# A selective scan that fetches its rows of C from memory instead of spreading them with TensorE

## The chip, the cores and the metric

The kernel runs on one core of a Trainium2 chip. The metric is the device time of one execution in microseconds (us). In this text PE is TensorE, DVE is VectorE, ACT is ScalarE, POOL is GpSimd and SP is the engine that here only issues DMAs. SBUF is the on-chip memory of 128 partitions, PSUM the memory that PE writes to, in eight banks of 512 float32 numbers per partition.

## The reference

Eight layers work one after the other on an activation x, seen here as 32 tiles of 128 tokens by 128 numbers. The change is in the fifth, a state-space layer. Cut to what it touches, per token t, channel d (256 channels) and state n (16 states):

```
xdbl = xc @ W_xproj                  # gives dt_r, B (16 numbers), C (16 numbers) per token
dt = softplus(dt_r @ W_dt + b_dt)
A = -exp(A_log)
h[t] = h[t-1] * exp(dt[t] * A) + dt[t] * B[t] * u[t]      # u is xc
y[t] = sum over n of h[t, n] * C[t, n]
out = x + ((y + xc * D_param) * silu(z)) @ W_out
```

All of it is float32.

## The kernel before, in words

The scan stage is the function `selective_scan` (L2628 to L3209). Tokens lie along the free dimension, channels on the partitions: 256 channels are two halves of 128 (`CH` = 2), and the tokens are cut into B = 8 groups q of S = 512, each with two sequences of 256. One turn m = 16 q + n handles state n of group q, so there are M = 128 turns, and nearly every operation of a turn is on 128 partitions by 1024 numbers. A turn has these steps:

1. SP fetches row n of B of the group from a scratch tensor in memory (`b_rows`) into all 128 partitions (L2707), 256 KB, into a ring of NB = 4 tiles `bs`. Before turn m it waits until the product of turn m - 4 is done.
2. POOL multiplies `dBu = du * bs` (L2770), into a ring of ND = 3, so it can be three turns ahead of the recurrence.
3. ACT computes the decay `dA = exp(dt * A)` in two calls (L2914) into PSUM banks 0 to 3, two turns ahead at most.
4. DVE runs the recurrence `h = dA * h + dBu` with one scan instruction (L3015), into a ring of NH = 5. One operand is in PSUM and one in SBUF.
5. h is weighed with row n of C. PE spreads that row to all partitions: it multiplies `pick`, a selection matrix, by `bc`, which holds B and C split into three bfloat16 parts whose sum is the float32 value (`spread`, L3122). The result is in PSUM bank 4 (`c_bank`), a single buffer, so the next spread waits until the weighing before it has read the bank. In 13 turns of 16, DVE weighs (`weigh`, L3024), with h in SBUF and C in PSUM. In turns with n = 0, 3 and 6, ACT copies the bank to SBUF (`take_c`, L2820) and POOL weighs (L2717), four turns later.
6. PE adds the weighed h to two PSUM banks `y_bank` through the identity matrix (`add_up`, L3139). The weighed tiles are in rings of NC = 3 (DVE's) and 2 (POOL's).

Every engine works through a list in a fixed order, with semaphores between them. DVE's order is recurrence m + 1, then weighing m, and once in each group `finish` (L3030) and `add` (L3036). POOL's is product m, then what the group needs once, then the weighing of m - 4 if it is POOL's.

Once in each group, work for the next ones is put between the turns: convolution, projection to B, C and the step sizes, gating, output. `take_bc` (L2859) on ACT copies the 32 rows of B and C out of PSUM to `raw` and stores the 16 rows of B to memory. The split into three parts takes three steps on ACT (`split_first` L2875, `split_mid` L2879, `split_done` L2883 and L2884) and two subtractions on POOL (`split_left` L2722, `split_last` L2726). The matrix `pick` is prepared on POOL in the first layer (L2615), ahead of the layer's own work for the next groups. `keep_running` (L3152) issues matmuls that serve no result. Each layer ends with a barrier over all engines.

Of the kernel before, what the change touches and what calls it, by code (L numbers as in the profile page):

```python
# [17 lines left out]
P = 128  # L18
# [2563 lines left out]
class ScanWeights:  # L2582
# [4 lines left out]
    def __init__(self, chip, ctx):  # L2587
        sb = lambda name, shape, dt=F32: chip.sb(ctx, f"scan_{name}", shape, dt)
        self.packed, self.w_dt = sb("packed", [P, self.WIDTH]), sb("w_dt", [R, DI])
        self.w_tap, self.pick = sb("w_tap", [P, TAPS, DI]), sb("pick", [P, N, P], BF16)  # L2590
# [37 lines left out]
def selective_scan(chip, held, answers):  # L2628
# [3 lines left out]
    PART = 32  # L2632
    NA, NB, ND, NH, NC = 2, 4, 3, 5, 3
# [3 lines left out]
    with ctx:  # L2637
# [5 lines left out]
        pick, d_diag, a_neg = held.pick, held.d_diag, held.a_neg  # L2643
# [9 lines left out]
        raw, dtr, left, mid = sb("raw", [2 * N, S]), sb("dtr", [R, S]), sb("left", [2 * N, S]), sb("mid", [2 * N, S], BF16)  # L2653
        bc = two("bc", [P, S], BF16)
        bs = [sb(f"bs{k}", [P, S]) for k in range(NB)]
        dBu, h, hc = ([sb(f"{n}{k}", [P, CH, S]) for k in range(c)] for n, c in (("dBu", ND), ("h", NH), ("hc", NC)))
        hp, c_rows = two("hp", [P, CH, S]), two("c_rows", [P, S])
        hp_ready, c_copied = sem("hp_ready"), sem("c_copied")
        dA = [chip.banks[:, CH * k:CH * (k + 1), :] for k in range(NA)]
        c_bank, y_bank = chip.psum[4], chip.psum[5:7]  # L2660
        b_rows = nc.dram_tensor("l2a_b_rows", (B, N, S), F32, kind="Internal").ap()
# [11 lines left out]
        for q in range(B):  # L2673
# [11 lines left out]
        xc_ready, sz_ready, hi_ready, raw_ready, left_ready, mid_ready, left2_ready, bc_ready = (  # L2685
            sem(n) for n in ("xc_ready", "sz_ready", "hi_ready", "raw_ready", "left_ready", "mid_ready", "left2_ready", "bc_ready"))
        log_ready, dt_ready, du_ready, exp_order = sem("log_ready"), sem("dt_ready"), sem("du_ready"), sem("exp_order")
        b_stored, edges = sem("b_rows_stored"), sem("edges_zeroed")
        b_loaded = [sem(f"b_loaded{k}") for k in range(NB)]
        dA_ready, dBu_ready, h_ready, C_ready, hc_ready, hc_summed, yT_ready = (  # L2690
            sem(n) for n in ("dA_ready", "dBu_ready", "h_ready", "C_ready", "hc_ready", "hc_summed", "yT_ready"))
        dve_order, cleared = sem("dve_order"), sem("bc_cleared")
# [4 lines left out]
        with nc.Block(no_gpsimd_drain=True) as block:  # L2697
            @block.sync
            def _(sp):
                answers.load(sp, (0,))  # L2700
                for m in range(M):
                    q, n = divmod(m, N)
                    if n == 0:
                        sp.wait_ge(b_stored, 16 * (q + 1))
                    if m >= NB:
                        sp.wait_ge(dBu_ready, m - NB + 1)
                    sp.dma_start(bs[m % NB][:], b_rows[q, n, :].partition_broadcast(P)).then_inc(b_loaded[m % NB], 16)  # L2707

            @block.gpsimd
            def _(pool):  # L2710
                def weigh(m):
                    k = pool_no[m]
                    pool.wait_ge(c_copied, k + 1)
                    pool.wait_ge(h_ready, m + 1)
                    if k >= 2:
                        pool.wait_ge(hc_summed, add_no[of_pool[k - 2]])
                    pool.tensor_tensor(hp[k % 2][:], h[m % NH][:], bcast(c_rows[k % 2][:], n_before=CH), ALU.mult).then_inc(hp_ready, 1)  # L2717

                def split_left(q):
                    pool.wait_ge(hi_ready, q + 1)  # L2720
                    pool.wait_ge(raw_ready, q + 1)
                    pool.tensor_tensor(left[:], raw[:], bc[q % 2][0:2 * N, :], ALU.subtract).then_inc(left_ready, 1)  # L2722

                def split_last(q):
                    pool.wait_ge(mid_ready, q + 1)
                    pool.tensor_tensor(left[:], left[:], mid[:], ALU.subtract).then_inc(left2_ready, 1)  # L2726
# [34 lines left out]
                split_left(0)  # L2761
                split_last(0)
                for m in range(M):
# [9 lines left out]
                    if q + 1 < B:  # L2773
                        if n == (5 if q else 7):
                            split_left(q + 1)
                        if n == 10:
                            split_last(q + 1)
# [8 lines left out]
            def _(act):  # L2786
# [27 lines left out]

                def take_c(m):
                    k = pool_no[m]
                    act.wait_ge(C_ready, m + 1)
                    if k >= 2:
                        act.wait_ge(hp_ready, k - 1)
                    act.copy(c_rows[k % 2][:], c_bank[:]).then_inc(c_copied, 1)  # L2820
# [38 lines left out]
                def take_bc(q):  # L2859
                    job = ("bc", q)  # L2860
                    bk.wait_filled(act, job, 0)
                    if q:
                        act.wait_ge(left2_ready, q)
                    act.copy(dtr[:], ps(job)[2 * N:2 * N + R, :]).then_inc(dtr_ready, 1)
                    if q:
                        act.wait_ge(b_stored, 16 * q)
# [3 lines left out]
                    act.dma_start(b_rows[q], raw[0:N, :]).then_inc(b_stored, 16)  # L2870

                def split_first(q):
                    if q >= 2:
                        act.wait_ge(C_ready, (q - 1) * N)
                    act.copy(bc[q % 2][0:2 * N, :], raw[:]).then_inc(hi_ready, 1)  # L2875

                def split_mid(q):
                    act.wait_ge(left_ready, q + 1)
                    act.copy(mid[:], left[:]).then_inc(mid_ready, 1)  # L2879

                def split_done(q):
                    act.wait_ge(left2_ready, q + 1)
                    act.copy(bc[q % 2][PART:PART + 2 * N, :], mid[:])  # L2883
                    act.copy(bc[q % 2][2 * PART:2 * PART + 2 * N, :], left[:]).then_inc(bc_ready, 1)  # L2884

# [43 lines left out]
                act.wait_ge(cleared, 1)  # L2929
                split_first(0)  # L2930
# [4 lines left out]
                split_mid(0)  # L2935
# [5 lines left out]
                split_done(0)  # L2941
                for m in range(M):
# [3 lines left out]
                    if m in pool_no:  # L2946
                        take_c(m)
# [6 lines left out]
                    if q + 1 < B:  # L2954
                        if n == 0 + late:
                            take_bc(q + 1)
                        if n == 1 + late:
                            split_first(q + 1)
# [4 lines left out]
                        if n == 6 + late:  # L2963
                            split_mid(q + 1)
                        if n == 7 + late:
                            log_dt(q + 1)
                        if n == 11 + late:
                            split_done(q + 1)
# [15 lines left out]
            def _(dve):  # L2984
# [33 lines left out]
                def weigh(m):  # L3018
                    k = dve_no[m]
                    dve.wait_ge(C_ready, m + 1)  # L3020
# [3 lines left out]
                    dve.tensor_tensor(hc[k % NC][:], h[m % NH][:], bcast(c_bank[:], n_before=CH), ALU.mult).then_inc(hc_ready, 1)  # L3024
# [14 lines left out]
                for u in range(2):  # L3039
                    ins = dve.memset(bc[u][:], 0.0)  # L3040
                ins.then_inc(cleared, 1)
# [32 lines left out]
            def _(pe):  # L3074
# [37 lines left out]
                def spread(m):  # L3112
                    if m >= M:
                        return
                    q, n = divmod(m, N)
                    if n == 0:
                        pe.wait_ge(bc_ready, q + 1)
                    if m - 1 in dve_no:
                        pe.wait_ge(hc_ready, dve_no[m - 1] + 1)
                    if m - 1 in pool_no:  # L3120
                        pe.wait_ge(c_copied, pool_no[m - 1] + 1)
                    pe.matmul(c_bank[:], pick[:, n, :], bc[q % 2][:], start=True, stop=True).then_inc(C_ready, 1)  # L3122

# [33 lines left out]
                keep_running(6, c_bank)  # L3157
# [5 lines left out]
                keep_running(1, c_bank)  # L3163
# [5 lines left out]
                keep_running(5, c_bank)  # L3169
                spread(0)  # L3170
                for m in range(M):
# [5 lines left out]
                    spread(m + 1)  # L3177
# [145 lines left out]
```

## Time and profile before

| | |
|---|---|
| median of 3 runs | 2709.16 us (2704.49 to 2710.79) |
| the profiled execution's own time | 2704.73 us |
| its span | 2703.0 us |
| busy over the span: PE, DVE, POOL, ACT | 2478.8, 1738.7, 1617.9, 1451.4 us |
| mean granted clock of TensorE | 0.959 |

The span is the time from the first to the last instruction, and busy time is time in which an engine executes something. Busy times of the engines overlap. The scan stage is about a sixth of the span, from the first product on POOL (L2770) at 834.13 us to the last weighing, which ends at 1269.02 us. A line of a group shows engine, operation, output and inputs with their shapes, the number of instructions, their busy time in us, the mean duration of one in ns, and after the second bar the idle time of the engine just before them and what ended it.

### The profile page before, as it was taken

What the parts mean: (1) busy time and instruction counts of PE and PEld (TensorE: products, weight loads), DVE (VectorE), ACT (ScalarE), POOL (GpSimd) and SP (SyncE); (2) the same over time, 40 slices, a digit from 0 to 9 for tenths busy, and PEclk for the clock granted to TensorE, in tenths of its full rate; (3) what the DMA queues carried; (4) which work ended last, traced back from release to release, by engine and by line L of the source; (5) the groups of instructions that cost most, each with busy time, mean ns of one, the idle gap of its engine ahead of it and who ended that gap; (6) DMA issues with size and microseconds to landing.
All of it is one profiled execution on the core that took longest, in us unless ns stands there. A gap on an engine that the chain in (4) does not pass through costs nothing. (4 is left out here: it accounts for less than half of the span.)

```text
span 2703.0 us, 42649 instructions
## 1 busy us (share of the span) xinstructions
PE 2478.8 (92%) x13288; PEld 1584.1 (59%) x13316; DVE 1738.7 (64%) x4099; ACT 1451.4 (54%) x2938; POOL 1617.9 (60%) x1421
## 2 busy tenths in 40 slices
PE   7995999997778999987499899999999999999999
PEld 4664998685763434433499544444444455777777
DVE  4436554764437999998666699999999981111112
ACT  2340443433458887774244577777777764343333
POOL 4652776531568999996255477677776761997000
PEclk9997999897899999999699899999999999999999
DMA  9010443401122222221701198888888882000001
GB/s 301 25 36 22 145 143 115 132 1 32 36 73 68 81 77 80 77 79 50 238 25 27 32 200 194 192 192 192 189 192 194 192 196 61 9 16 9 9 8 32
DMA packets 144678, 268.33 MB, mean 99 GB/s; under 512 B 28491, under 2 KB 68310, under 8 KB 144454
## 3 DMA queue, kind: packets, MB, share of 16 engines
q1 hardware_dynamic: 132342, 245.45, 35.4%
q0 software_dynamic: 9088, 18.63, 2.5%
q8 instruction: 109, 1.79, 0.3%
q10 hardware_dynamic: 3024, 1.52, 0.2%
q14 instruction: 115, 0.94, 0.1%
HBM read 96.74 MB, written 24.32 MB: 45 GB/s over the span
## 5 line engine op out<-in xcount | busy, mean ns | idle before, releaser
L1775 POOL TENSOR_TENSOR l3a_p_all<-l3a_p_all,l3a_rden 128x1024 f32<-128x1024 f32 x256 | 483.8, 1894 | 202.9 <-DVE l3a_rden L1850 202.8
L1908 ACT ACTIVATE l3a_p_all<-l3a_p_all,l3a_low 128x512 f32<-128x512 f32 x512 | 364.3, 713 | 130.9 <-DVE l3a_low L1845 129.6
L1845 DVE CUSTOM_DVE_ANT_0 l3a_p_all<-bank,relative_bias 128x512 f32<-128x512 f32 x512 | 331.8, 686 | 55.1 <-PE bank L1974 31.4
L1858 DVE STREAM_TRANSPOSE l3a_blocks<-l3a_p_all 128x1024 f32<-128x1024 f32 x256 | 313.9, 1235 | 1.8 <-issue 1.8
L2770 POOL TENSOR_TENSOR l2a_dBu<-l2a_du,l2a_bs 128x1024 f32<-128x1024 f32 x128 | 298.5, 2352 | 17.6 <-DVE l2a_h L3015 15.4
L3015 DVE TENSOR_TENSOR_SCAN l2a_h<-bank,l2a_dBu 128x1024 f32<-128x1024 f32 x128 | 290.8, 2280 | 13.8 <-POOL l2a_dBu L2770 7.8
L1832 DVE SCALAR_TENSOR_TENSOR x<-bank,l3a_blocks,x 128x128 f32<-128x128 f32 x256 | 71.9, 344 | 336.5 <-PE bank L2049 336.3
L1923 ACT ACTIVATE relative_bias<-bank,l3a_b 128x512 f32<-128x512 f32 x224 | 153.0, 688 | 214.4 <-PE bank L2039 210.8
L1974 PE MATMUL bank<-l3a_kT,l3a_qT 64*128 64x512 f32 x1024 | 244.4, 604 | 4.0 <-DVE l3a_low L1845 3.5
L2000 PE MATMUL bank<-l3a_pT,l3a_v 128*64 128x512 f32 x1024 | 233.8, 598 | 0.1
L2039 PE MATMUL bank<-relative_xnT_all,relative_w_qk 128*128 128x512 f32 x512 | 230.4, 594 | 0.0
L2049 PEld LDWEIGHTS bank<-relative_w_qk,relative_bias 128*128 128x128 f32 x1792 | 208.1, 192 | 25.1 <-issue 25.1
L2049 PE MATMUL bank<-relative_w_qk,relative_bias 128*128 128x128 f32 x1792 | 208.5, 275 | 1.0 <-DVE x L1832 1.0
L3139 PE MATMUL bank<-l2a_hc,ident 128*128 128x512 f32 x416 | 201.2, 607 | 2.6 <-DVE l2a_hc L3024 1.5
L2914 ACT ACTIVATE bank<-l2a_dt,scan_a_neg 128x511 f32<-128x511 f32 x256 | 165.1, 680 | 53.7 <-DVE l2a_h L3015 49.9
L1974 PEld LDWEIGHTS bank<-l3a_kT,l3a_qT 64*128 64x128 f32 x1024 | 97.8, 187 | 150.2 <-issue 138.1
L2039 PEld LDWEIGHTS bank<-relative_xnT_all,relative_w_qk 128*128 128x128 f32 x512 | 92.9, 191 | 93.5 <-issue 93.5
L2000 PEld LDWEIGHTS bank<-l3a_pT,l3a_v 128*64 128x64 f32 x1024 | 67.8, 136 | 120.1 <-issue 111.9
L1980 PE MATMUL bank<-relative_xnT_all,relative_w_qk 128*128 128x512 f32 x256 | 128.7, 626 | 2.9 <-issue 2.9
L3024 DVE TENSOR_TENSOR l2a_hc<-l2a_h,bank 128x1024 f32<-128x1024 f32 x104 | 124.5, 1198 | 2.6 <-PE bank L3122 1.3
L3139 PEld LDWEIGHTS bank<-l2a_hc,ident 128*128 128x128 f32 x416 | 81.6, 196 | 76.1 <-issue 72.4
L1415 POOL DMA_INDIRECT l2fc_xs<-l2f_xn_rows,l2f_source x64 | 67.5, 1054 | 85.0 <-POOLq L868 38.9
(529 smaller groups left out, 4995.8 us busy)
## 6 DMA issues: line engine op xcount, KB each, us to landing
l3a_pT<-l3a_blocks SPq DMA_DIRECT2D x1024, 128.0 KB, 2.4
l2a_bs<-l2a_b_rows SPq DMA_DIRECT2D x128, 256.0 KB, 3.1
l0fe_wv<-expert_weights SPq DMA_DIRECT2D x71, 256.0 KB
by_place<-by_distance SPq DMA_DIRECT2D x16, 512.0 KB, 12.5
relative_bias<-by_place SPq DMA_DIRECT2D x16, 448.0 KB, 11.1
expert_weights<-in_L_ffn_in_dram SPq DMA_DIRECT2D x1, 4096.0 KB, 29.0
l0f_answers<-l0f_y_rows SPq DMA_DIRECT2D x16, 256.0 KB, 5.2
relative_w_qk<-in_L_ffn_W_dram SPq DMA_DIRECT2D x16, 256.0 KB, 3.2
```

The source lines that it names most:

```text
L1775: p_ready.by(pool.tensor_tensor(a, a, bcast(rden[g % 2][:, t, :], n_after=S), ALU.mult))
L1845: bk.drain(dve.tensor_tensor_reduce(p_of(g, t)[:, h, :], ps(job)[:], bias[:, u * 2 + h, b0:b0 + S], 1.0, 3.0e38, ALU.add, ALU.min, low[:, ...
L1858: ins = dve.transpose(out, p_of(g, t).rearrange("p h (k b j) -> p (h k) b j", b=Q, j=32))
L1908: ins = act.activation(a, a, ACT.Exp, bias=low[:, t, h:h + 1], scale=-1.0, accum_out=den[:, t, h:h + 1])
L1974: bk.fill(pe.matmul(ps(job)[:], qT[half[h], t * P:(t + 1) * P], kT[half[h], :], start=True, stop=True), job)
L2000: ins = pe.matmul(ps(job)[half[h], :], v[g // GP % 2][:, kt, c:c + DK3], pT[g % 2][:, :, h * TPS + kt, :], start=(kt == 0), stop=(kt == TP ...
L2039: bk.fill(pe.matmul(ps(job)[:], w1[e % 2][:, j * P:(j + 1) * P], xnT_all[:, q * S:(q + 1) * S], start=True, stop=True), job)
L2049: ins = pe.matmul(ps(job)[:, t * D:(t + 1) * D], h[q][:, j, t * P:(t + 1) * P], w2[e % 2][:, j, :], start=(j == 0), stop=(j == J - 1))
L2770: pool.tensor_tensor(dBu[m % ND][:], du[q % 2][:], bcast(bs[m % NB][:], n_before=CH), ALU.mult).then_inc(dBu_ready, 1)
L2914: ins = act.activation(dA[m % NA][:, j, 1:], dt[q % 2][:, j, 1:], ACT.Exp, scale=a_neg[:, j, n:n + 1])
L3015: dve.tensor_tensor_scan(h[m % NH][:].rearrange("p c s -> p (c s)"), dA[m % NA].rearrange("p c s -> p (c s)"), dBu[m % ND][:].rearrange("p ...
L3139: ins = pe.matmul(y_bank[j][:], chip.ident[:], weighed[:, j, :], start=False, stop=(m % N == N - 1))
```

## The change

Rows of C take the way of the rows of B. `take_bc` stores all 32 rows to memory, and SP fetches each row of C to all partitions into a ring of NK = 6 tiles `cs` in SBUF, two turns behind the row of B. Its fetch for turn k waits for the weighing of turn k - 6. DVE and POOL both weigh with `cs`. The three parts, `pick`, the spreading matmuls, ACT's copies, and what synchronised them are gone.

```diff
@@ ScanWeights.prepare
-        pool.tensor_copy(self.pick[:], bcast(self.part_of[:, N:2 * N], n_after=P))
@@ selective_scan
-    NA, NB, ND, NH, NC = 2, 4, 3, 5, 3
+    NA, NB, ND, NH, NC, NK, BEHIND = 2, 4, 3, 5, 3, 6, 2
...
-        b_rows = nc.dram_tensor("l2a_b_rows", (B, N, S), F32, kind="Internal").ap()
+        bc_rows = nc.dram_tensor("l2a_bc_rows", (B, 2 * N, S), F32, kind="Internal").ap()
@@ SP
-                for m in range(M):
-                    q, n = divmod(m, N)
-                    if n == 0:
-                        sp.wait_ge(b_stored, 16 * (q + 1))
-                    if m >= NB:
-                        sp.wait_ge(dBu_ready, m - NB + 1)
-                    sp.dma_start(bs[m % NB][:], b_rows[q, n, :].partition_broadcast(P)).then_inc(b_loaded[m % NB], 16)
+                for m in range(M + BEHIND):
+                    if m < M:
+                        q, n = divmod(m, N)
+                        if n == 0:
+                            sp.wait_ge(bc_stored, 16 * (q + 1))
+                        if m >= NB:
+                            sp.wait_ge(dBu_ready, m - NB + 1)
+                        sp.dma_start(bs[m % NB][:], bc_rows[q, n, :].partition_broadcast(P)).then_inc(b_loaded[m % NB], 16)
+                    k = m - BEHIND
+                    if k >= 0:
+                        if k - NK in dve_no:
+                            sp.wait_ge(hc_ready, dve_no[k - NK] + 1)
+                        if k - NK in pool_no:
+                            sp.wait_ge(hp_ready, pool_no[k - NK] + 1)
+                        sp.dma_start(cs[k % NK][:], bc_rows[k // N, N + k % N, :].partition_broadcast(P)).then_inc(c_loaded[k % NK], 16)
@@ POOL: weigh (split_left and split_last and their calls are removed)
-                    pool.wait_ge(c_copied, k + 1)
+                    pool.wait_ge(c_loaded[m % NK], 16 * (m // NK + 1))
...
-                    pool.tensor_tensor(hp[k % 2][:], h[m % NH][:], bcast(c_rows[k % 2][:], n_before=CH), ALU.mult).then_inc(hp_ready, 1)
+                    pool.tensor_tensor(hp[k % 2][:], h[m % NH][:], bcast(cs[m % NK][:], n_before=CH), ALU.mult).then_inc(hp_ready, 1)
@@ ACT: take_bc (take_c, split_first, split_mid, split_done and their calls are removed)
...
-                    act.dma_start(b_rows[q], raw[0:N, :]).then_inc(b_stored, 16)
+                    act.wait_ge(raw_ready, q + 1)
+                    act.dma_start(bc_rows[q], raw[:]).then_inc(bc_stored, 16)
@@ DVE: weigh (the clearing of bc is removed)
-                    dve.wait_ge(C_ready, m + 1)
+                    dve.wait_ge(c_loaded[m % NK], 16 * (m // NK + 1))
...
-                    dve.tensor_tensor(hc[k % NC][:], h[m % NH][:], bcast(c_bank[:], n_before=CH), ALU.mult).then_inc(hc_ready, 1)
+                    dve.tensor_tensor(hc[k % NC][:], h[m % NH][:], bcast(cs[m % NK][:], n_before=CH), ALU.mult).then_inc(hc_ready, 1)
@@ PE (spread and its calls are removed)
-                    pe.matmul(c_bank[:], pick[:, n, :], bc[q % 2][:], start=True, stop=True).then_inc(C_ready, 1)
```

## Rows read from the trace of the kernel before

**Rows 1.** Busy time by stretch: before, in and after the scan stage.

```profile
core 0: us, PE busy (x) PEld busy (x) DVE busy (x) ACT busy (x) POOL busy (x), PEclk, DMA share, GB/s
834.13:1269.02 434.89, 394.07 (x1014) 169.74 (x1032) 413.56 (x254) 329.38 (x505) 401.30 (x183) 0.98 0.24 76
```

**Rows 2.** Who waited for whom, 836 to 1272 us: total us, times, longest.

```profile
POOL l2a_dBu L2770 <- DVE l2a_h L3015: 15.4, 14, 1.6
...
DVE l2a_h L3015 <- POOL l2a_dBu L2770: 7.8, 5, 2.2
...
DVE l2a_h L3015 <- ACT bank L2914: 5.8, 13, 0.8
...
POOL l2a_hp L2717 <- PE bank L3139: 4.8, 5, 1.2
...
DVE l2a_hc L3024 <- PE bank L3122: 1.3, 6, 0.2
```

**Rows 3.** Groups of instructions by line, 836 to 1272 us.

```profile
L2770 POOL TENSOR_TENSOR l2a_dBu<-l2a_du,l2a_bs 128x1024 f32<-128x1024 f32 x128 | 298.5, 2352 | 17.6 <-DVE l2a_h L3015 15.4 <-DVE l2a_du L3055 1.2 <-PE bank L3139 0.9
L3015 DVE TENSOR_TENSOR_SCAN l2a_h<-bank,l2a_dBu 128x1024 f32<-128x1024 f32 x128 | 290.8, 2280 | 13.8 <-POOL l2a_dBu L2770 7.8 <-ACT bank L2914 5.8
...
L3024 DVE TENSOR_TENSOR l2a_hc<-l2a_h,bank 128x1024 f32<-128x1024 f32 x104 | 124.5, 1198 | 2.6 <-PE bank L3122 1.3 <-remote 1.2
...
L2717 POOL TENSOR_TENSOR l2a_hp<-l2a_h,l2a_c_rows 128x1024 f32<-128x1024 f32 x24 | 56.4, 2352 | 4.9 <-PE bank L3139 4.8
...
L2736 POOL TENSOR_TENSOR l2a_du<-l2a_dt,l2a_xc 128x1024 f32<-128x1024 f32 x7 | 16.5, 2360 | 0.0
...
L2726 POOL TENSOR_TENSOR l2a_left<-l2a_left,l2a_mid 32x512 f32<-32x512 f32 x7 | 8.0, 1148 | 1.2 <-ACT l2a_mid L2879 1.2
```

**Rows 4.** Order of time at 846 us: start us, us, then the instruction.

```profile
846.65 2.35 POOL L2717 TENSOR_TENSOR l2a_hp<-l2a_h,l2a_c_rows 128x1024 f32<-128x1024 f32 x1
846.72 1.20 DVE L3024 TENSOR_TENSOR l2a_hc<-l2a_h,bank 128x1024 f32<-128x1024 f32 x1
```

**Rows 5.** Order of time, DVE and POOL, 830 to 841 us.

```profile
830.66 1.23 DVE L3047 TENSOR_TENSOR l2a_dt<-l2a_dt,l2a_work 128x1024 f32<-128x1024 f32 x1 [5.94 <-ACT l2a_work L2901]
...
831.22 1.68 POOL L2726 TENSOR_TENSOR l2a_left<-l2a_left,l2a_mid 32x512 f32<-32x512 f32 x1 [5.17 <-ACT l2a_mid L2879]
...
831.92 2.06 DVE L3055 TENSOR_TENSOR l2a_du<-l2a_dt,l2a_xc 128x1024 f32<-128x1024 f32 x1
...
834.13 6.97 POOL L2770 TENSOR_TENSOR l2a_dBu<-l2a_du,l2a_bs 128x1024 f32<-128x1024 f32 x3 [1.23 <-DVE l2a_du L3055]
```

**Rows 6.** Order of time, DVE and POOL, 815 to 817.3 us.

```profile
815.50 1.44 DVE L1001 SCALAR_TENSOR_TENSOR x<-expert_weights,l1f_answer_gates,x 128x128 f32<-128x128 f32 x1
815.52 1.27 POOL L2746 TENSOR_TENSOR x<-x,expert_weights 128x512 f32<-128x512 f32 x1
...
816.77 0.49 POOL L2744 TENSOR_SCALAR expert_weights<-expert_weights,l1f_answer_gates,zeros 128x128 f32<-128x128 f32 x1
```

**Rows 7.** The line of that DVE instruction: ns min/median/max of its 20.

```profile
L1001 DVE SCALAR_TENSOR_TENSOR x<-expert_weights,l1f_answer_gates,x x20: 343/348/1441, 804.8 to 817.9; 128x128 f32<-128x128 f32 x20
```

**Rows 8.** Fetches of B rows: time on SP's queue in ns, and to landing.

```profile
L2707 SPq DMA_DIRECT2D l2a_bs<-l2a_b_rows x128: 319/320/432, 825.4 to 1248.1; - x128
...
DMA to landing us min/median/max: 3.0/3.1/4.1
```

**Rows 9.** Order of time, the last weighing and what follows it.

```profile
1267.80 1.22 DVE L3024 TENSOR_TENSOR l2a_hc<-l2a_h,bank 128x1024 f32<-128x1024 f32 x1 [1.16 <-remote]
1271.23 1.29 DVE L3030 TENSOR_TENSOR l2a_sz<-bank,l2a_sz 128x512 f32<-128x512 f32 x2 [2.21 <-PE bank L3139]
```

**Rows 10.** Matmuls that add weighed tiles: ns min/median/max.

```profile
L3139 PE MATMUL bank<-l2a_hc,ident x416: 590/592/1061, 848.8 to 1270.6; 128*128 128x512 f32 x139
```

**Rows 11.** Order of time in the first layer, POOL and DVE.

```profile
89.32 1.90 POOL L2615 CAST scan_pick<-scan_packed 128x2048 bf16<-128x2048 f32 x1
...
95.53 1.29 DVE L358 TENSOR_TENSOR l0a_qk<-l0a_qkv,l0a_inv 128x512 f32<-128x512 f32 x2 [3.12 <-POOL l0a_inv L284]
```

More of the change, by code:

```diff
@@ L2589, in __init__ @@
         self.packed, self.w_dt = sb("packed", [P, self.WIDTH]), sb("w_dt", [R, DI])
-        self.w_tap, self.pick = sb("w_tap", [P, TAPS, DI]), sb("pick", [P, N, P], BF16)
+        self.w_tap = sb("w_tap", [P, TAPS, DI])
         self.d_diag, self.a_neg = sb("d_diag", [P, CH, P]), sb("a_neg", [P, CH, N])
@@ L2642, in selective_scan @@
         ln_w, ln_b, conv_b, b_dt = held.ln_w, held.ln_b, held.conv_b, held.b_dt
-        pick, d_diag, a_neg = held.pick, held.d_diag, held.a_neg
+        d_diag, a_neg = held.d_diag, held.a_neg
         both_eps, warm = sb("both_eps", [P, 1]), sb("warm", [P, 1])
@@ L2652, in selective_scan @@
         dt, du = two("dt", [P, CH, S]), two("du", [P, CH, S])
-        raw, dtr, left, mid = sb("raw", [2 * N, S]), sb("dtr", [R, S]), sb("left", [2 * N, S]), sb("mid", [2 * N, S], BF16)
-        bc = two("bc", [P, S], BF16)
-        bs = [sb(f"bs{k}", [P, S]) for k in range(NB)]
+        raw, dtr = sb("raw", [2 * N, S]), sb("dtr", [R, S])
+        bs, cs = ([sb(f"{n}{k}", [P, S]) for k in range(c)] for n, c in (("bs", NB), ("cs", NK)))
         dBu, h, hc = ([sb(f"{n}{k}", [P, CH, S]) for k in range(c)] for n, c in (("dBu", ND), ("h", NH), ("hc", NC)))
-        hp, c_rows = two("hp", [P, CH, S]), two("c_rows", [P, S])
-        hp_ready, c_copied = sem("hp_ready"), sem("c_copied")
+        hp, hp_ready = two("hp", [P, CH, S]), sem("hp_ready")
         dA = [chip.banks[:, CH * k:CH * (k + 1), :] for k in range(NA)]
-        c_bank, y_bank = chip.psum[4], chip.psum[5:7]
-        b_rows = nc.dram_tensor("l2a_b_rows", (B, N, S), F32, kind="Internal").ap()
+        spare_bank, y_bank = chip.psum[4], chip.psum[5:7]
+        bc_rows = nc.dram_tensor("l2a_bc_rows", (B, 2 * N, S), F32, kind="Internal").ap()
         M = B * N
@@ L2684, in selective_scan @@
         mv_ready, gains_ready, rows_ready, x_normed = sem("mv_ready"), sem("gains_ready"), sem("rows_ready"), sem("x_normed")
-        xc_ready, sz_ready, hi_ready, raw_ready, left_ready, mid_ready, left2_ready, bc_ready = (
-            sem(n) for n in ("xc_ready", "sz_ready", "hi_ready", "raw_ready", "left_ready", "mid_ready", "left2_ready", "bc_ready"))
+        xc_ready, sz_ready, raw_ready = (sem(n) for n in ("xc_ready", "sz_ready", "raw_ready"))
         log_ready, dt_ready, du_ready, exp_order = sem("log_ready"), sem("dt_ready"), sem("du_ready"), sem("exp_order")
[L2688 to L2692, printed above, removed]
+        bc_stored, edges = sem("bc_rows_stored"), sem("edges_zeroed")
+        b_loaded, c_loaded = ([sem(f"{n}_loaded{k}") for k in range(c)] for n, c in (("b", NB), ("c", NK)))
+        dA_ready, dBu_ready, h_ready, hc_ready, hc_summed, yT_ready = (
+            sem(n) for n in ("dA_ready", "dBu_ready", "h_ready", "hc_ready", "hc_summed", "yT_ready"))
+        dve_order = sem("dve_order")
         inverted = sem("inverted")
@@ L2716, in weigh @@
                         pool.wait_ge(hc_summed, add_no[of_pool[k - 2]])
-                    pool.tensor_tensor(hp[k % 2][:], h[m % NH][:], bcast(c_rows[k % 2][:], n_before=CH), ALU.mult).then_inc(hp_ready, 1)
[L2719 to L2726, printed above, removed]
+                    pool.tensor_tensor(hp[k % 2][:], h[m % NH][:], bcast(cs[m % NK][:], n_before=CH), ALU.mult).then_inc(hp_ready, 1)
                 def add_step(q, part):
@@ L2773, in _ @@
                     if q + 1 < B:
[L2774 to L2777, printed above, removed]
                         if n == 12:
@@ L2861, in take_bc @@
                     bk.wait_filled(act, job, 0)
-                    if q:
-                        act.wait_ge(left2_ready, q)
                     act.copy(dtr[:], ps(job)[2 * N:2 * N + R, :]).then_inc(dtr_ready, 1)
                     if q:
-                        act.wait_ge(b_stored, 16 * q)
+                        act.wait_ge(bc_stored, 16 * q)
                     bk.drain(act.copy(raw[:], ps(job)[0:2 * N, :]), job)
@@ L2869, in take_bc @@
                     act.sem_inc(raw_ready, 1)
-                    act.dma_start(b_rows[q], raw[0:N, :]).then_inc(b_stored, 16)
[L2872 to L2884, printed above, removed]
+                    act.wait_ge(raw_ready, q + 1)
+                    act.dma_start(bc_rows[q], raw[:]).then_inc(bc_stored, 16)
                 def take_dt(q, j):
@@ L2934, in _ @@
                 log_dt(0)
-                split_mid(0)
                 deviations(2)
@@ L2940, in _ @@
                     decay(m)
-                split_done(0)
                 for m in range(M):
@@ L2956, in _ @@
                             take_bc(q + 1)
-                        if n == 1 + late:
-                            split_first(q + 1)
                         if n in (3 + late, 4 + late):
@@ L2962, in _ @@
                             exp_dt(q + 1)
-                        if n == 6 + late:
-                            split_mid(q + 1)
                         if n == 7 + late:
                             log_dt(q + 1)
-                        if n == 11 + late:
-                            split_done(q + 1)
                     if q + 2 < B:
@@ L3038, in _ @@
                 dve.memset(both_eps[:], LN_EPS * LN_EPS)
-                for u in range(2):
-                    ins = dve.memset(bc[u][:], 0.0)
-                ins.then_inc(cleared, 1)
                 for k in range(2):
@@ L3156, in _ @@
                 bk.open(pe)
-                keep_running(6, c_bank)
+                keep_running(6, spare_bank)
                 turn(0)
@@ L3162, in _ @@
                 turn(1)
-                keep_running(1, c_bank)
+                keep_running(1, spare_bank)
                 project(0)
@@ L3168, in _ @@
                     conv(1, j, range(TAPS))
-                keep_running(5, c_bank)
-                spread(0)
+                keep_running(5, spare_bank)
                 for m in range(M):
```

24 lines of the change are left out of this document (removed).

## The prediction

> **What bounds the kernel now.** The layers run one after the other with a barrier between them, so the change is worth what it does to the scan stage, and the stage is read by itself. I took the busy time by stretch first. The stage lasts 434.9 us, from the first product to the last weighing, and in it DVE is busy 413.6 us and POOL 401.3 us [rows 1]. These two bind together, and neither has room: 21 us on DVE, 34 us on POOL. The waits say how they hang together. POOL waits 15.4 us in all for the recurrence (its ring of three is full), and DVE waits 7.8 us for products and 5.8 us for decays [rows 2], so DVE sets the pace, at 434.9 / 8 = 54.4 us for a group of 16 turns. What C costs today hardly shows: DVE waits 1.3 us in all for the spreading matmul [rows 2], and 1.2 us once at the very end [rows 9]. PE shows 394 us busy [rows 1], but ends almost none of DVE's waits. By their counts, a group has on POOL 16 products, 3 weighings and two products for the step sizes, and on DVE 16 recurrences and 13 weighings [rows 3].
>
> **What the weighing becomes.** This edit decides the sum. Today DVE weighs h (SBUF) with C (PSUM). Beside a POOL operation that runs the whole time it takes 1.20 us, and the POOL operation takes its usual 2.35 us [rows 4]: neither notices the other. After the change both inputs of the weighing are in SBUF. The trace of before has such instructions on DVE, and a few of them meet POOL:
> - At 831.92 DVE starts `du` (two SBUF inputs, 128x1024). A POOL subtraction is running and ends at 831.22 + 1.68 = 832.90. The DVE instruction takes 2.06 us, to 833.98, which is 1.08 us after POOL's end. The same shape just before it took 1.23 us [rows 5].
> - That one, at 830.66, was running when the POOL subtraction started, and ended at 831.89. POOL then needed until 832.90, 1.01 us more, and its record is 1.68 us where its kind has a mean of 1.148 [rows 3, 5].
> - At 815.50 a DVE instruction of two SBUF tensors, whose median is 0.348 us [rows 7], takes 1.44 us, to 816.94. The POOL operation beside it ends at 816.79. The next POOL operation was queued right behind and started at 816.77, yet DVE was through 0.15 us after the first one's end [rows 6].
>
> So a DVE instruction with two SBUF inputs and a POOL operation don't run side by side. Whichever comes second waits for the first, the wait is inside its record, and it finishes after the first one's end plus its own time less about 0.15 us (1.23 - 1.08 = 0.15; 1.148 - 1.01 = 0.14 [rows 3, 5]). The third case shows that a waiting DVE instruction gets in between two POOL operations, so it isn't locked out while POOL has work.
>
> The Trainium skill has this as a rule, in "SBUF — State Buffer", "Who interferes with whom": a DVE instruction with two SBUF inputs contends with a GpSimd instruction that reads SBUF, and one blocks the other for its whole length. The trace agrees that they exclude each other; on the length it is about 0.15 us kinder per handover. By the rule's whole lengths the sum below would be 518 us instead of 485 us.
>
> **The sum for the stage.** POOL's operations and DVE's weighings now queue for one thing, so their times add.
> - POOL operations of 128x1024: 128 products, 24 weighings, 7 `du`, and 7 additions for `dt` of the same shape: 166 [rows 3]. Back to back they follow each other every (6.97 - 2.35) / 2 = 2.31 us [rows 3, 5]: 166 x 2.31 = 383.5 us.
> - 104 weighings on DVE [rows 3], each now sandwiched between POOL operations. Each adds 1.08 us, and shortens the POOL operation behind it from 2.31 to 2.35 - 0.14 = 2.21 us: 104 x (1.08 - 0.10) = 101.9 us.
> - Together 485.4 us; for a full group 21 x 2.31 + 13 x 0.98 = 61.3 us against 54.4 us now. The recurrence (2.28 us, one input in PSUM [rows 3]) doesn't take part: it runs beside the POOL operation that follows each weighing, and the two are of one length, 2.2 us. DVE then comes to its next weighing just as POOL ends, and the queue is never empty. I followed one group with these durations and the orders of both engines: after one group POOL is the later engine, DVE waits for products, and a group takes 61.4 us.
> - At the end nothing is left on POOL while DVE does the last recurrence: 2.3 us. For moments in which neither uses the turn (a late decay, today 5.8 us in all, and POOL's wait for PE's sums, 4.8 us [rows 2]) I put 5 us; bounds 0 and 15.
>
> **The other edits of the stage.**
> - Start: the POOL subtraction in front of `du` goes, so DVE no longer loses 2.06 - 1.23 = 0.8 us there [rows 5]; with a cast less on ACT, 1.3 us (bounds 0.8 and 2). The first product starts at 834.1 - 1.3 = 832.8.
> - The last spreading matmul (1.2 us [rows 9]) and the 1.3 us of waits for it [rows 2] are hidden in the new queue; a bound of -2.5 us. A weighing by itself goes from 1.198 to 1.226 us, which is inside the 1.08.
> - POOL's two subtractions per group (7 x 2 x 1.15 = 16 us [rows 3]) go. They read SBUF too, so without the change they would be in the queue; here they are simply absent, and already left out of the 166.
> - ACT loses 24 copies and four small operations per group. It isn't the bound: 329 of 435 us [rows 1]. Nothing.
> - PE loses 128 spreading matmuls. It doesn't set the pace, so nothing; but its pauses grow (see the rivals).
> - DMA: 128 more fetches of 256 KB. SP's queue gives 0.32 us to each, 0.64 of 3.4 us per turn. A fetch lands after 3.1 us (4.1 at most) [rows 8] with the DMA engines 24% busy [rows 1], which becomes under 50%. SP issues B of turn m once product m - 4 is done, so it has three products, over 7 us, to land. Before B of turn m + 1, SP now waits for weighing m - 8 and issues C of m - 2. On POOL that weighing stands right behind product m - 4, ahead of product m - 3 for which SP waits anyway; on DVE it is older than what product m - 4 needed. Then C has about five turns until it is used. So nothing is late; a fetch would have to take over twice its time. The store of 64 KB instead of 32 KB happens a group ahead.
>
> New end of the last weighing: 832.8 + 485.4 + 2.3 + 5 = 1325.5, against 1269.0: +56.5 us. What follows it (`finish`, output, barrier) is unchanged [rows 9].
>
> **First layer.** The 1.90 us cast on POOL goes; DVE waited 3.12 us for POOL shortly behind it [rows 11]. Bounds 0 and -1.9; PE is busy there, so I take -1.0.
>
> Sum: +55.5 us. The profiled execution took 2704.7 us, so 2760.2; the median of the runs shown is 4.5 us above it. I say 2762.
>
> **Rivals.**
> - Operands don't meet (the other side). It rests on three encounters of other tiles, and rows of B read by POOL never met a two-input DVE instruction with an operand repeated over the halves. If the weighing stays at 1.2 us beside a running POOL operation, the stage keeps DVE's pace and gains the start (1.3), the waits for C (2.5), and up to 5 us of waits for products, since POOL has 16 us less to do; it loses 104 x 0.03 = 3 us. With the first layer's 1.0 that is about -7 at best, -3 likely: 2702. What decides is whether the median record of the weighing stays near 1.2 us. Chance 0.11.
> - Whole lengths. If in a long queue each operation holds the other off for its full record, nothing of the 0.15 us is saved: 166 x 2.352 + 104 x 1.226 = 518 us [rows 3, 5], 32.5 us more, 2793. Against it speak both handovers of [rows 5]. Chance 0.07. This is the length that the Trainium skill gives ("SBUF — State Buffer", "Who interferes with whom").
> - DVE and POOL out of step. Each weighing comes at a random moment of a POOL operation and waits 1.15 us on average. Then DVE is bound by itself: 16 x 2.28 + 13 x (1.08 + 1.15) + 1.29 for `finish` [rows 3, 9] = 66.8 us for a group, 8 x 66.8 = 534 us, +100 us: 2805. For it: finish and add push DVE off the beat. Against: a full ring makes POOL wait for h and puts them in step again. Chance 0.07.
> - PE's clock. The stage has 0.98 of the full clock now [rows 1], PE spends less in a longer stage, and an adding matmul goes from 592 to 1061 ns at the half clock [rows 10]. PE has 394 us of records in 435 us [rows 1], and twice that would bind. Pauses are shorter than a group's, and once behind, PE has no pauses, so I see dips and not a state: 2775 to 2790. Chance 0.04.
> - Fetches late, SP bound: over 7 us to landing. Chance 0.01.
> - My forecast: 0.70, by itself 2745 to 2780.
>
> Less than 0.2% (5.4 us) can't be told from no change. Faster by more needs the first rival at its better half: 0.06. Same: 0.05. Slower: 0.89. The range 2738 to 2800 leaves out the first rival and most of the third.
>
> **What would show it.** The weighing's record (L3024): minimum about 1.2, median 1.3 or more, many up to 3.5 us. Products (L2770): often 2.35 + up to 1.1 us, mean near 2.9. In the waits, DVE's recurrence behind POOL's product grows from 7.8 us to tens, and POOL's wait for the recurrence shrinks. Time per group 61 us. Fetches of B still land in 3 to 4 us. Wrong: a median weighing of 1.2 us with POOL busy beside it, or waits of either for `cs` or `bs`.

## The result, and the profile after

The change makes the kernel slower: 2771.36 us median of 4 runs (2766.97 to 2773.48) against 2709.97 us of 4 runs before. The ratio is 1.0225, 95% interval 1.0206 to 1.0244, that is 56 to 66 us. The forecast was 2762 us, with a range of 2738 to 2800.

The profiled execution after has a span of 2771.7 us and took 2773.48 us. First the busy time of the scan stage, from the first product to the last weighing, in the columns of [rows 1]:

```profile
core 0: us, PE busy (x) PEld busy (x) DVE busy (x) ACT busy (x) POOL busy (x), PEclk, DMA share, GB/s
840.61:1338.50 497.89, 404.09 (x907) 168.43 (x906) 468.03 (x254) 301.71 (x451) 483.21 (x169) 0.91 0.41 133
```

The stage takes 497.9 us instead of 434.9. POOL has 14 instructions fewer and is busy 82 us longer: 483 of 498 us. So POOL is now the engine that never rests. The groups of instructions say how, beside [rows 3]:

```profile
L2762 POOL TENSOR_TENSOR l2a_dBu<-l2a_du,l2a_bs 128x1024 f32<-128x1024 f32 x128 | 368.2, 2900 | 16.7 <-DVE l2a_du L3006 12.7 <-PE bank L3078 1.5 <-DVE l2a_h L2969 1.3
L2969 DVE TENSOR_TENSOR_SCAN l2a_h<-bank,l2a_dBu 128x1024 f32<-128x1024 f32 x128 | 291.1, 2278 | 26.7 <-POOL l2a_dBu L2762 20.8 <-ACT bank L2880 5.1
...
L2978 DVE TENSOR_TENSOR l2a_hc<-l2a_h,l2a_cs 128x1024 f32<-128x1024 f32 x104 | 179.8, 1730 | 0.0
...
L2720 POOL TENSOR_TENSOR l2a_hp<-l2a_h,l2a_cs 128x1024 f32<-128x1024 f32 x24 | 77.3, 3219 | 5.0 <-PE bank L3078 5.0
```

The recurrence, with one operand in PSUM, is as long as before (2278 against 2280 ns). The product went from 2352 to 2900 ns, POOL's weighing from 2352 to 3219, DVE's from 1198 to 1730. The mean hides how the wait is shared. The lines of DVE's weighing and of the product (min/median/max in ns) show it:

```profile
L2978 DVE TENSOR_TENSOR l2a_hc<-l2a_h,l2a_cs x104: 1192/1196/3402, 849.9 to 1337.3; 128x1024 f32<-128x1024 f32 x104
```

```profile
L2762 POOL TENSOR_TENSOR l2a_dBu<-l2a_du,l2a_bs x128: 2330/3328/3367, 840.6 to 1329.6; 128x1024 f32<-128x1024 f32 x128
```

Most of DVE's weighings still take 1.2 us. It is POOL's product that mostly waits, 1.0 us each time. The order of time shows both cases:

```profile
854.04 1.20 DVE L2978 TENSOR_TENSOR l2a_hc<-l2a_h,l2a_cs 128x1024 f32<-128x1024 f32 x1
854.09 3.36 POOL L2720 TENSOR_TENSOR l2a_hp<-l2a_h,l2a_cs 128x1024 f32<-128x1024 f32 x1
855.16 2.28 DVE L2969 TENSOR_TENSOR_SCAN l2a_h<-bank,l2a_dBu 128x1024 f32<-128x1024 f32 x1
857.41 6.94 POOL L2762 TENSOR_TENSOR l2a_dBu<-l2a_du,l2a_bs 128x1024 f32<-128x1024 f32 x3
859.84 2.29 DVE L2969 TENSOR_TENSOR_SCAN l2a_h<-bank,l2a_dBu 128x1024 f32<-128x1024 f32 x1 [2.40 <-POOL l2a_dBu L2762]
862.04 3.39 DVE L2978 TENSOR_TENSOR l2a_hc<-l2a_h,l2a_cs 128x1024 f32<-128x1024 f32 x1
864.32 3.32 POOL L2720 TENSOR_TENSOR l2a_hp<-l2a_h,l2a_cs 128x1024 f32<-128x1024 f32 x1
```

At 854.04 DVE starts 0.05 us ahead of POOL and takes 1.20 us; POOL's operation ends at 857.45, 2.21 us after DVE's end. That pair is the one of [rows 4], where both ran at full speed. At 862.04 DVE comes second. POOL's third product ends at 857.41 + 6.94 = 864.35, and the weighing at 865.43, 1.08 us later. POOL's next operation had started its record at 864.32 and took 3.32 us, so DVE got in between.

The waits of the stage turned round, beside [rows 2]:

```profile
DVE l2a_h L2969 <- POOL l2a_dBu L2762: 20.8, 9, 2.4
...
DVE l2a_h L2969 <- ACT bank L2880: 5.1, 3, 3.6
POOL l2a_hp L2720 <- PE bank L3078: 5.0, 2, 2.9
```

POOL's wait for the recurrence fell from 15.4 to 1.3 us, and DVE's for the product rose from 7.8 to 20.8. Neither DVE nor POOL waits for a fetched row anywhere in the stage. The fetches of B land after 3.3 us (before 3.1), those of C after 3.6:

```profile
l2a_bs<-l2a_bc_rows SPq DMA_DIRECT2D x128, 256.0 KB, 3.3
l2a_cs<-l2a_bc_rows SPq DMA_DIRECT2D x128, 256.0 KB, 3.6
```

In the profiled pair the spans differ by 68.7 us, more than the 61.4 us of the medians. The stage gives 63.0 of it. Some 7 us lie in the third layer, which the change doesn't touch. Counted from the start of that layer's statistics to that of the next layer's, it took 157.7 us in the profiled execution before and 164.9 after, but in three of the runs below, in which the kernel before took 2706 us, it took 157.2, 165.0 and 165.9. That is scatter between executions and not the change.

### The profile page after: what moved, and what is told of

Read it like the earlier page. It is cut to its first block and busy times, and to the rows that moved or that the text cites. A ratio compares the mean times of both kernels' runs of the same rounds, so it can differ in the third digit from the quotient of the medians.

```text
span 2771.7 us, 42430 instructions
## 1 busy us (share of the span) xinstructions
PE 2492.6 (90%) x13188; PEld 1584.1 (57%) x13188; DVE 1792.8 (65%) x4097; ACT 1422.6 (51%) x2882; POOL 1694.6 (61%) x1404
## 5 line engine op out<-in xcount | busy, mean ns | idle before, releaser
L2762 POOL TENSOR_TENSOR l2a_dBu<-l2a_du,l2a_bs 128x1024 f32<-128x1024 f32 x128 | 368.2, 2900 | 16.7 <-DVE l2a_du L3006 12.7
L2969 DVE TENSOR_TENSOR_SCAN l2a_h<-bank,l2a_dBu 128x1024 f32<-128x1024 f32 x128 | 291.1, 2278 | 26.7 <-POOL l2a_dBu L2762 20.8
L3078 PE MATMUL bank<-l2a_hc,ident 128*128 128x512 f32 x416 | 230.0, 684 | 59.6 <-DVE l2a_hc L2978 59.6
L2978 DVE TENSOR_TENSOR l2a_hc<-l2a_h,l2a_cs 128x1024 f32<-128x1024 f32 x104 | 179.8, 1730 | 0.0
```

The lines of the kernel that those rows point to most:

```text
L2762: pool.tensor_tensor(dBu[m % ND][:], du[q % 2][:], bcast(bs[m % NB][:], n_before=CH), ALU.mult).then_inc(dBu_ready, 1)
L2969: dve.tensor_tensor_scan(h[m % NH][:].rearrange("p c s -> p (c s)"), dA[m % NA].rearrange("p c s -> p (c s)"), dBu[m % ND][:].rearrange("p ...
L2978: dve.tensor_tensor(hc[k % NC][:], h[m % NH][:], bcast(cs[m % NK][:], n_before=CH), ALU.mult).then_inc(hc_ready, 1)
L3078: ins = pe.matmul(y_bank[j][:], chip.ident[:], weighed[:, j, :], start=False, stop=(m % N == N - 1))
```

## The experiments

All ratios are to the kernel before, run beside each experiment. It took 2706 us beside some and 2787 to 2794 beside others, where the layers ahead of the stage take some 70 us longer, so whole times are compared as ratios. "Stage" is always from the first product to the last weighing, in one profiled execution.

**Operand in PSUM again.** The kernel after, fetches and all, but DVE's second operand comes from PSUM.

```diff
-  dve.tensor_tensor(hc[k % NC][:], h[m % NH][:], bcast(cs[m % NK][:], n_before=CH), ALU.mult)
+  dve.tensor_tensor(hc[k % NC][:], h[m % NH][:], bcast(spare_bank[:], n_before=CH), ALU.mult)
```

> The kernel after, but DVE's weighing takes its second operand from PSUM bank 4, which is filled once at the start, instead of from the fetched row in SBUF. All fetches of C rows, their waits, POOL's weighings and everything else stay. Left out: on DVE's turns the value of C (it multiplies by fixed numbers). Theory (a DVE instruction with two SBUF inputs and a POOL operation exclude each other): the exclusion is gone, POOL's product goes back to 2.35 us and the weighing to 1.20, first product to last weighing takes about 430 us instead of 498, time about 2705 (2698 to 2714). Rival 1 (the 128 extra fetches or the stores cost the time): nothing changes, 2765 to 2775. Rival 2 (TensorE, with less to do and a lower granted clock in this stage, costs it): the spreading matmuls are still missing, so the clock stays low and at least 15 us of the loss remains, 2725 or more.

Measured: ratio 0.9964 (0.9948 to 0.9979), 10 us faster than before. The stage takes 423.3 us:

```profile
L2979 DVE TENSOR_TENSOR l2a_hc<-l2a_h,bank x104: 1191/1192/1211, 914.9 to 1327.7; 128x1024 f32<-128x1024 f32 x104
```

```profile
L2762 POOL TENSOR_TENSOR l2a_dBu<-l2a_du,l2a_bs x128: 2332/2355/2387, 905.6 to 1316.9; 128x1024 f32<-128x1024 f32 x128
```

With the operand in PSUM both medians and both maxima are back where they were, and the whole loss is gone, with all 256 fetches still made and all spreading matmuls still missing. That fells the rivals of the fetches and of less work for TensorE. The granted clock of this stage is 0.97, so the run says nothing on a low clock by itself. It also shows what the removal of the spreading and splitting is worth when nothing is paid for it, and nothing waits for a row in the bank: 10 us.

**Operand in SBUF, nothing else.** The kernel before, with a fixed tile in SBUF as DVE's second operand.

```diff
+  c_fixed, c_set = sb("c_fixed", [P, S]), sem("c_set")
...
-  dve.tensor_tensor(hc[k % NC][:], h[m % NH][:], bcast(c_bank[:], n_before=CH), ALU.mult)
+  dve.tensor_tensor(hc[k % NC][:], h[m % NH][:], bcast(c_fixed[:], n_before=CH), ALU.mult)
```

> The kernel before, but DVE's weighing takes its second operand from a tile in SBUF that is set once, instead of from the PSUM bank. The spreading matmuls, the three parts, ACT's copies and all waits stay, and no row of C is fetched. Left out: on DVE's turns the value of C. Theory (exclusion): the whole loss appears with this edit alone. The kernel also has POOL's 14 small subtractions, each some 1 us in the same queue: stage about 500 to 515 us, time 2770 to 2785. Rivals (fetches; less work for TensorE): nothing changes, 2705 to 2714.

Measured: ratio 1.0416 (1.0385 to 1.0447), about +114 us; stage 551.4 us, 69 us for a group. The sign is the theory's, the size is not: I had expected 60 to 75 us. The weighing's line shows what I had not thought of, and the order of time shows one case:

```profile
L3026 DVE TENSOR_TENSOR l2a_hc<-l2a_h,l2a_c_fixed x104: 1191/1198/13780, 914.1 to 1454.9; 128x1024 f32<-128x1024 f32 x104
```

```profile
1069.73 4.64 POOL L2771 TENSOR_TENSOR l2a_dBu<-l2a_du,l2a_bs 128x1024 f32<-128x1024 f32 x2
1073.19 6.87 DVE L3026 TENSOR_TENSOR l2a_hc<-l2a_h,l2a_c_fixed 128x1024 f32<-128x1024 f32 x1
1074.33 2.34 POOL L2718 TENSOR_TENSOR l2a_hp<-l2a_h,l2a_c_rows 128x1024 f32<-128x1024 f32 x1
1076.64 2.34 POOL L2771 TENSOR_TENSOR l2a_dBu<-l2a_du,l2a_bs 128x1024 f32<-128x1024 f32 x1
1079.99 2.28 DVE L3016 TENSOR_TENSOR_SCAN l2a_h<-bank,l2a_dBu 128x1024 f32<-128x1024 f32 x1
1082.18 1.19 DVE L3026 TENSOR_TENSOR l2a_hc<-l2a_h,l2a_c_fixed 128x1024 f32<-128x1024 f32 x1
1082.41 3.19 POOL L2771 TENSOR_TENSOR l2a_dBu<-l2a_du,l2a_bs 128x1024 f32<-128x1024 f32 x1 [3.43 <-DVE l2a_h L3016]
```

The weighing's record starts at 1073.19 (below: DVE asks), and DVE sees three operations of POOL end (1074.37, 1076.67, 1078.98) before its weighing ends, 1.08 us after the last of them. Only then, with its ring full, POOL waits 3.43 us for the recurrence, and that time is lost. This happens to 8 of the 104 weighings, which take 6.9 to 13.8 us; without them every weighing ends within one operation of POOL.

**The same without POOL's subtractions.** The kernels before and after also differ in POOL's list, so the run above was repeated with POOL's list of the kernel after.

```diff
   def split_left(q):
...
+      if q:
+          pool.sem_inc(left_ready, 1)
+          return
       pool.tensor_tensor(left[:], raw[:], bc[q % 2][0:2 * N, :], ALU.subtract).then_inc(left_ready, 1)
```

(`split_last` alike. Group 0 keeps both subtractions; they stand ahead of the stage.)

> The run in which the kernel before weighs from a fixed tile in SBUF took 114 us more than before, not 60 to 75: 69 us for a group. In 8 of its 104 weighings DVE waited out 3 to 6 operations of POOL in a row. Here the same kernel leaves out POOL's two subtractions for groups 1 to 7 (their values, and on DVE's turns the value of C, are left out), so POOL's list is that of the kernel after. Nothing is fetched for C. Theory: with POOL's list of the kernel after the time is that of the kernel after too, 61.6 us for a group, ratio 1.021 to 1.027, which would show that the fetches have no part in the loss. Rival (the fetches or their waits keep DVE and POOL in step, and without them DVE is starved): long weighings stay, over 65 us for a group, ratio above 1.033.

Measured: ratio 1.0236 (1.0215 to 1.0258), stage 497.5 us, against 1.0225 and 497.9 us of the kernel after. No weighing is over 3.4 us:

```profile
L3032 DVE TENSOR_TENSOR l2a_hc<-l2a_h,l2a_c_fixed x104: 1192/1196/3396, 844.0 to 1331.0; 128x1024 f32<-128x1024 f32 x104
```

This kernel fetches no C, and it keeps the spreading matmuls, ACT's copies and ACT's part of the split. The place of one operand, with POOL's list equal, makes the whole of the time, within the intervals. That the two stages agree to 0.4 us is in part chance: most groups take 61.8 us here and 61.6 in the kernel after, and the longer ones differ (64.2 us for the seventh here, 65.9 for the second there).

**POOL weighs less, in both kernels.** One edit, made to the kernel after and to the kernel before:

```diff
-        SHARED, LATER, ADDED_AT = (0, 3, 6), 4, {0: 6, 3: 12, 6: 13}
+        SHARED, LATER, ADDED_AT = (0,), 4, {0: 6, 3: 12, 6: 13}
```

> The kernel after, with POOL weighing one turn of 16 (n = 0) instead of three; DVE weighs 15 instead of 13. The result is complete. Theory: POOL's operation holds the other off for 2.31 us and DVE's weighing for 0.98 us net, so the queue gets shorter by 16 x (2.31 - 0.98) = 21 us although DVE gets more work: 2750 (2745 to 2758). Rival (DVE itself is the bound, as in the forecast's case of both out of step, and waits about half a POOL operation per weighing): slower, by 16 x 1.1 to 2.2 us = 18 to 35 us, 2789 to 2806. Rival (fetches set the pace): no change, 2771.

> The kernel before, with the same edit as the run ahead of it: POOL weighs one turn of 16 instead of three. The result is complete. Theory: here nothing excludes anything, DVE sets the pace and gets 16 weighings of 1.11 us (start to start) more: +18 us, less the waits for POOL that go (up to 7 us): 2720 to 2729. The same edit that shortens the kernel after lengthens the kernel before. If the queue were the same in both, it would be faster here too.

Measured: after, 1.0165 (1.0137 to 1.0193), against 1.0225 without the edit, about 16 us less; the stage is 477.8 us, 20.1 us shorter, where the sum of the queue said 21. Before, 1.0022 (1.0011 to 1.0032), about 6 us more; the stage is 443.6 us, 8.7 us longer. I had expected 11 to 20 us more there, so this one misses its range: more of DVE's extra work was hidden than I thought, and where isn't shown. The stages of both runs are set against stages profiled at another time. The sign differs between the two kernels, as the theory needs: after, what counts is the sum of POOL's operations and DVE's weighings, and a weighing on DVE takes less of the queue than one on POOL; before, DVE's own time counts. Both out of step, with DVE bound by itself, would have been slower in both.

**Looking for a version that beats both.** The first experiment had 10 us to give. One way fetches C for POOL's turns alone, the other fetches all of it and lets ACT copy DVE's rows to PSUM.

```diff
# kernel before, SP: a row of C for POOL's turns; PE: spread(m) for DVE's turns alone
+  if m in pool_no:
+      k = pool_no[m]
+      if k >= 3:
+          sp.wait_ge(hp_ready, k - 2)
+      sp.dma_start(c_rows[k % 3][:], b_rows[q, N + n, :].partition_broadcast(P)).then_inc(c_loaded[k % 3], 16)
```

> The kernel before, with rows of C fetched from memory (ring of 3) for POOL's three turns of 16 alone. PE spreads only for DVE's 13 turns, and ACT's 24 copies are gone. DVE still weighs from PSUM. The result is complete. Theory: no exclusion, DVE sets the pace, and it gains what ACT's late decays and the waits for the bank cost, of which the trace of before shows 5.8 + 2.6 us: ratio to before 0.997 to 1.000. Rival (fetches cost time): above 1.002.

Measured: 0.9996 (0.9982 to 1.0009): no difference. The stage is 2.8 us shorter in its profile, too little to show. The waits that were to go are still there: DVE waits 6.1 us for decays (5.8 before) and 2.9 us for the bank.

```diff
# kernel after, ACT, behind decay(m + NA)
+  if m in dve_no:
+      k = dve_no[m]
+      act.wait_ge(c_loaded[m % NK], 16 * (m // NK + 1))
+      if k:
+          act.wait_ge(hc_ready, k)
...
+      act.copy(spare_bank[:], cs[m % NK][:]).then_inc(C_ready, 1)
```

> The kernel after, with its fetches, but ACT copies the fetched row to PSUM bank 4 in each of DVE's 104 turns, and DVE weighs from there. POOL weighs from the fetched tile. The result is complete. Theory: the exclusion is gone as in the run with fixed numbers in the bank (0.9964); ACT gets 104 x 0.58 = 60 us more on 301, which leaves it under 370 of 423 us, so it isn't the bound, but a copy can be late where ACT does its once-in-a-group work, since there is one bank: ratio to before 0.9965 to 1.002. If the gain of that run came from fixed numbers in the bank and not from what was removed, this one stays above 1.00. If a copy is often late, the weighing waits for ACT, and the ratio goes to 1.005 and over.

Measured: 1.0058 (1.0041 to 1.0074). All records are short again (no weighing over 1.3 us), so with real rows too the bank takes the exclusion away. But the third case of the expectation came true; of the waits of the stage:

```profile
POOL l2a_dBu L2762 <- DVE l2a_h L2977: 42.8, 35, 4.5
DVE l2a_hc L2986 <- ACT bank L2915: 31.5, 20, 3.4
```

DVE waits 31.5 us for copies, 27 of them at n = 14, 15, 8 and 4, where ACT also does the group's work. The stage is 449.4 us. The last two runs let DVE weigh some of those turns straight from the fetched tile.

```diff
+  DIRECT = (14, 15)          # second run: (4, 8, 14, 15)
+  banked = {m: k for k, m in enumerate(m for m in of_dve if m % N not in DIRECT)}
...
+  dve.tensor_tensor(hc[k % NC][:], h[m % NH][:], bcast(spare_bank[:] if m in banked else cs[m % NK][:], n_before=CH), ALU.mult)
```

> The run with ACT's copies to PSUM came to 1.0058 of before: DVE waited 31.5 us for late copies, at n = 14 and 15 of nearly every group (2.2 and 1.3 us), and at 4, 5 and 8. Here DVE weighs the turns n = 14 and 15 straight from the fetched tile in SBUF, the other 11 of its 13 from the bank. The result is complete. Theory: these waits go (some 23 us). What the two turns cost in their place is small as long as DVE sets the pace: POOL waits for the recurrence, so DVE's weighing starts first, and it is POOL that waits 1.0 us, of which it has slack. Ratio to before 0.996 to 1.000. If exclusion costs DVE half a POOL operation in each such turn (1.1 us x 16 = 18 us), the ratio is 1.003 or more.

> The same, with the turns n = 4, 8, 14 and 15 straight from SBUF and 9 from the bank. The result is complete. Theory: another 10 us of late copies go, against 16 more operations of POOL that wait 1.0 us each; POOL has 423 - 386 = 37 us of slack in the stage and this uses 32 of it: ratio 0.994 to 1.000, near the 0.9964 of the kernel whose bank was filled once. If the queue counts from the first such weighing on, it is slower than the kernel with two of them.

Measured: 1.0035 (1.0021 to 1.0049) and 1.0052 (1.0032 to 1.0072). Both miss their ranges. With two turns direct, the weighing at n = 14 takes 1.2 us and waits for nothing, as expected, but only 9 us of the waits for copies went. The expectation had put 23 us on these two turns; the trace of the run before has 16.4 (n = 14 waits in six groups, n = 15 in two). And waits moved: DVE still waits 22.3 us for copies, half of it at n = 4 (1.7 to 3.1 us).

```profile
DVE l2a_hc L2990 <- ACT bank L2916: 22.3, 15, 3.1
```

This ratio lies where the expectation put a DVE that waits half a POOL operation, but no weighing from SBUF took over 1.23 us, so that isn't the cause. With four, the wait for copies is 4.7 us, but the weighing at n = 8 takes 3.2 us in seven groups of eight, because there POOL's product is already running, and the one at n = 4 takes 1.5. So a weighing from SBUF was free only where DVE came first. The intervals of the two runs overlap, so which of them is slower stays open. No version with a complete result that I ran beats the kernel before.

## Why the prediction was right

- **The exclusion.** Right. It was read from three encounters in the trace of before [rows 5, 6], and the runs with the operand in PSUM and in SBUF show that it is the whole effect. Handovers measure as forecast: 1.08 us after POOL's end, 2.21 us after DVE's. The length is the row's and not the full record; that rival had 2793 us. The Trainium skill ("SBUF — State Buffer", "Who interferes with whom") calls the pair of ports that DVE and GpSimd share an exclusive lock, and says that it is held "for the whole instruction" of DVE's modes that read one tensor through two ports. Here each handover is some 0.15 us shorter than that.
- **The sum of the queue.** Forecast 485.4 + 2.3 + 5 = 492.7 us from the first product to the last weighing, measured 497.9. A full group was worked out at 61.4 us and takes 61.6: the recurrences that open two groups stand at

```profile
1095.44 2.28 DVE L2969 TENSOR_TENSOR_SCAN l2a_h<-bank,l2a_dBu 128x1024 f32<-128x1024 f32 x1
...
1157.07 2.28 DVE L2969 TENSOR_TENSOR_SCAN l2a_h<-bank,l2a_dBu 128x1024 f32<-128x1024 f32 x1
```

  The missing 5 us are in the first two groups, which take 63.2 and 65.9 us. The 5 us for idle moments of the queue were too few; 10 would have been right, inside the bounds of 0 and 15. POOL's waits of the stage lie in these groups too: 6.5 us for PE's sums and 1.3 us for a recurrence. This is the one term that was mis-sized, and most of why +55.5 us fell 6 us short of the +61.4 us of the medians. The forecast of 2762 lies another 3 us lower than its own sum, which gives 2764.7 from the median of 2709.2.
- **Who waits.** Half wrong. I wrote that the median weighing would take 1.3 us or more; it stayed at 1.196. By my own working, recurrence and product run side by side and are both 2.2 us long, so who comes first is decided by hundredths. DVE wins mostly, by 0.05 us in the rows above, and the wait stands in POOL's records. The mean of the product, 2900 ns against "near 2.9", came out right. The sign to look for was the wait of the pair, not that of the weighing: by my text a median of 1.2 with POOL busy beside it would have spoken against the forecast, and it was no evidence of that.
- **A waiting DVE gets its turn.** Right for the kernel after: none of its 104 weighings saw POOL take a further turn ahead of it. As a general statement it was wrong. It rested on one case of 0.35 us [rows 6], and with one other list of POOL 8 of 104 weighings lost two turns or more, and their records are together 46 us longer than after a wait for one operation. Had the kernel after met that (+114 us), it would have been outside my range. That it didn't was luck: nothing in the working told the two lists apart.
- **The start of the stage.** POOL's subtraction in front of `du` is gone, and `du` took 1.22 us instead of 2.06. From the stage's first statistics to the first product it is 27.1 us against 28.1 before, -1.1 by the unrounded times for a forecast of -1.3.
- **First layer.** -1.0 us forecast, -0.2 measured (the second layer's first gather starts at 260.3 against 260.5). In the other runs it starts anywhere from 258.2 to 261.3, so a difference of 1 us can't be read there.
- **TensorE.** The granted clock of the stage fell from 0.98 to 0.91, in dips, as the rival had it. From the third group on it costs nothing: in that group, for one, POOL is busy 61.47 of 61.60 us (the columns are those of [rows 1]). In the first two groups it does cost something. PE had no matmul from 860 to 865 us; from 864 to 877 the granted clock was 0.50, four adding matmuls took 3.78 us instead of 1.88, and POOL waited 2.89 us for the sum of its weighed tile:

```profile
864.00:877.00 13.00, 11.51 (x16) 4.60 (x17) 12.91 (x7) 6.49 (x11) 11.57 (x5) 0.50 0.46 151
972.20:1033.80 61.60, 50.83 (x121) 21.30 (x120) 59.18 (x33) 39.43 (x60) 61.47 (x22) 0.94 0.42 138
```

```profile
871.20 3.78 PE L3078 MATMUL bank<-l2a_hc,ident 128*128 128x512 f32 x4
875.63 2.65 PE L3078 MATMUL bank<-l2a_hp,ident 128*128 128x512 f32 x4
878.12 1.88 PE L3078 MATMUL bank<-l2a_hc,ident 128*128 128x512 f32 x4
878.46 2.35 POOL L2720 TENSOR_TENSOR l2a_hp<-l2a_h,l2a_cs 128x1024 f32<-128x1024 f32 x1 [2.89 <-PE bank L3078]
```

  The kernel with the operand in SBUF and all spreading matmuls has a clock of 0.95 and about the same time, so it is a matter of a few us at most. No run changed the clock alone.
- **Fetches.** Right: nothing waits for them, and the run with PSUM operand is faster than before with all of them.
- **The rival on the other side** (operands don't meet, 2702) is what the first experiment measures: 0.9964, about 2700.

## What to carry to other kernels

When an operand of a VectorE instruction moves from PSUM to SBUF and its other input is in SBUF too, add its time to GpSimd's and compare the sum with the stage: here 125 + 401 us against 435. The trace of before held three such meetings, and the longest record of an otherwise constant line (1.44 us where the median is 0.348 [rows 6, 7]) was where to look. If the sum doesn't fit, try shifting work to the engine that holds the other off for less time: here 0.98 us for a weighing on DVE against 2.31 us for one on POOL, and moving 16 of them shortened the stage by 20 us.

## What I had not expected of the hardware

- A VectorE instruction that waits for GpSimd can lose several turns in a row: up to six GpSimd operations ended within one record of 13.78 us. In all eight cases it asked 1.0 to 1.2 us after the start of a GpSimd operation, with more of them queued. But in the kernel after it asked at the same distance seven times and got the next turn each time. The traces show one difference: in all eight, the operation that was running or the next one was a weighing of POOL; in those seven, in six more of the same run and in seven each of two other runs, a product was running and a product or a subtraction came next. No run tests whether that is what decides, so it stays open.
- In every meeting shown here the wait is inside the record of the engine that waits, and not in its idle time. The list of waits shows little of it: DVE's idle time before the recurrence grew from 13.8 to 26.7 us and POOL's wait for it shrank, while the stage grew by 63 us.
